# A decoder on one core: the second half's routing moved into both expert stages, and the last product rows sent directly

## The reference, cut to what matters

```python
x = _layernorm(x + _L0_attn_ref(x, ...))      # 16 heads, causal
x = _layernorm(x + _L0_xattn_ref(x, ctx_1024, ...))
x = _layernorm(x + _L0_ffn_ref(x, ...))       # experts, two of eight per token
x = _layernorm(x + _L1_attn_ref(x, ...))      # a memory matrix, updated 64 times in turn
x = _layernorm(x + _L1_xattn_ref(x, ...))     # a GELU feed-forward per sequence
x = _layernorm(x + _L1_ffn_ref(x, ...))       # experts, one of eight per token
```

```python
topk_scores, topk_idx = jax.lax.top_k(scores, k)            # first layer, k = 2
topk_probs = jax.nn.softmax(topk_scores, axis=-1)
idx = jnp.argmax(probs, axis=-1); gate = jnp.max(probs, axis=-1)   # second layer
```

## Time and profile before

| what | us |
|---|---|
| median of 3 runs (1908.21 to 1913.42) | 1910.16 |
| the profiled execution, its own time | 1911.16 |
| its span, first to last instruction | 1909.4 |

### The profile page before, as it was taken

One profiled execution on the slowest core, in us unless ns is written; L12 is line 12 of the kernel. 1 busy time (PEld: TensorE's weight loads), 2 busy tenths in 40 slices (PEclk: granted clock), 3 DMA queues, 4 the chain that ended last, 5 costly groups with the idle time before them and its releaser, 6 DMA issues. The chain is left out here.

```text
span 1909.4 us, 59731 instructions
## 1 busy us (share of the span) xinstructions
PE 1317.5 (69%) x18142; PEld 1072.6 (56%) x18196; DVE 1314.9 (69%) x4812; ACT 1104.9 (58%) x3182; POOL 1036.1 (54%) x1500
## 2 busy tenths in 40 slices
PE   6999995988878846996690999600001787849990
PEld 4677763666656636996580677400001665639990
DVE  5999995677788764542565666488886577755575
ACT  4777773677766735774472555354444565636674
POOL 2777775333326775777772344225542453867663
PEclk9999998899999978998795999855555898979995
DMA  2444442311112222333454254400000421323344
GB/s 75 106 114 106 114 115 77 107 51 50 50 42 69 79 63 73 95 91 92 126 144 146 66 111 89 82 1 1 0 1 17 149 79 51 84 70 86 89 116 118
DMA packets 201497, 152.38 MB, mean 80 GB/s; under 512 B 20482, under 2 KB 188802, under 8 KB 200962
## 3 DMA queue, kind: packets, MB, share of 16 engines
q1 hardware_dynamic: 188034, 123.13, 24.3%
q0 software_dynamic: 13312, 27.49, 4.4%
HBM read 76.54 MB, written 65.54 MB: 74 GB/s over the span
## 5 line engine op out<-in xcount | busy, mean ns | idle before, releaser
L1119 PE MATMUL ffn_run_up_ps<-ffn_run_xt,ffn_run_w_now 128*128 128x128 f32 x1792 | 248.3, 283 | 49.4 <-DVE ffn_run_h L1247 19.8
L1089 POOL DMA_INDIRECT expert_outputs<-ffn_run_y_all,ffn_run_ids x224 | 219.3, 979 | 86.8 <-issue 45.5
L1119 PEld LDWEIGHTS ffn_run_up_ps<-ffn_run_xt,ffn_run_w_now 128*128 128x128 f32 x1792 | 223.8, 196 | 61.2 <-ACT ffn_run_xt L1155 33.0
L838 POOL DMA_INDIRECT tokens_by_expert<-ffn_x_all,ffn_dest x192 | 190.7, 993 | 53.4 <-issue 49.1
L392 POOL TENSOR_TENSOR cross_k_ex<-cross_kt,k_pack 128x256 f32<-128x256 f32 x128 | 76.7, 621 | 193.0 <-ACT cross_kt L591 192.9
L1128 PE MATMUL ffn_run_y_ps<-ffn_weights,ffn_run_h 128*128 x1216 | 173.6, 277 | 0.9 <-DVE ffn_run_y_all L1264 0.5
L1599 POOL TENSOR_TENSOR recur_parts<-ffn_weights,recur_cv 128x62 f32<-128x62 f32 (+30 forms) x62 | 93.4, 1507 | 146.0 <-DVE recur_cv L1676 146.0
L1843 PE MATMUL mixer_m_ps<-mixer_mine,mem_state_coef 128*64 128x64 f32 x4 | 0.5, 334 | 246.4 <-DVE mixer_off_in L1980 246.4
L1128 PEld LDWEIGHTS ffn_run_y_ps<-ffn_weights,ffn_run_h 128*128 128x128 f32 x1216 | 154.9, 193 | 1.3 <-issue 1.3
L1156 ACT COPY ffn_run_w_now<-ffn_weights 128x512 f32 x224 | 139.4, 622 | 0.0
L1843 PEld LDWEIGHTS mixer_m_ps<-mixer_mine,mem_state_coef 128*64 128x64 f32 x4 | 0.3, 204 | 246.5 <-DVE mixer_ones L1978 246.5
(11 more groups left out here) (329 smaller groups left out, 4553.0 us busy)
## 6 DMA issues: line engine op xcount, KB each, us to landing
ffn_run_x<-tokens_by_expert SPq DMA_DIRECT2D x56, 260.0 KB, 3.0
tokens_by_expert<-fill_zeros SPq DMA_DIRECT2D x32, 292.5 KB, 2.8
ffn_run_yg<-expert_outputs SPq DMA_DIRECT2D x16, 512.0 KB, 4.6
memory_rows<-products_row SPq DMA_DIRECT2D x16, 390.0 KB, 4.5
ffn_weights<-memory_rows SPq DMA_DIRECT2D x16, 390.0 KB
tokens_by_expert<-fill_zeros SPq DMA_DIRECT2D x32, 162.5 KB, 2.6
ffn_weights<-in_pack_ffn SPq DMA_DIRECT2D x1, 4112.0 KB, 14.1
self_turned<-in_x_turned SPq DMA_DIRECT2D x64, 64.0 KB, 1.8
```

The lines of the kernel that those rows point to most:

```text
L838: pool.indirect_dma_start(xs[h], bass.IndirectOffsetOnAxis(ap=self.dest[:, r, t:t + 1], axis=0), self.x_all[:, t, :], None)\
L1089: pool.indirect_dma_start(ys, bass.IndirectOffsetOnAxis(ap=ids[:, t:t + 1], axis=0), y_all[:, t, :], None)\
L1119: mm = nc.tensor.matmul(up_ps[t.slot(2)][:, c * P:(c + 1) * P], w_now[:, t.slot(2), c * P:(c + 1) * P], xt[:, t.slot(2), :], start=True, s ...
```

## The change

The second half's routing leaves cross attention and the mixer. In `run_experts` DVE takes four of its operations per step, two ahead of the step's own first operation and two ahead of the output, from step -3 to step 15; the counts are copied and `place` begins at step 3. PE counts at the end of step 0, in an accumulator bank of its own. ACT takes the exponentials at step 3 (stage 0) or -2 (stage 1). POOL sends the outputs of tiles 0 to 7, waits for the routing (in stage 0 for the gates too), then scatters, then goes on with output 8. Three engines wait by `experts_known` for the second half's expert numbers. In stage 0 `START` goes from tile 96 to tile 108, and the roots stand nine outputs apart.

In the products the last four tiles' rows go from their buffer to `room` directly, two DMAs per tile (64 rows of 195 numbers each); the reads back come a step earlier; the wait for them moves from SP ahead of the barrier to ACT and DVE in the recurrence. ACT takes a square root at the end of the products into a column that nothing reads.

```diff
             else:
                 half_way(dve, step, 4, 4, Tile, middle, peeled=8)
                 pull(64)
-                f.route(dve, back, 1)
...
-    START = MID + (24 if top2 else 8)
+    START = MID + (36 if top2 else 8)
+    ROOTS, APART = (START + 2, 9) if top2 else (START + 5, 8)
+    EARLY = 8
...
-            for n in range(K * HALF):
-                f.scatter(pool, xs, 1, n)
             for t in range(kind.ALL):
+                if t == EARLY:
+                    pool.wait_ge(f.routed, 2)
+                    for n in range(K * HALF):
+                        f.scatter(pool, xs, 1, n)
                 pool.wait_ge(y_copied, t + 1)
...
+                if i.static and i.c == 0:
+                    f.count_tokens(pe, counts, 1)
-            skewed(pe, step, 3, 0, kind)
+            skewed(pe, step, 3, 0, kind, pause=(MID, lambda: pe.wait_ge(f.experts_known, 2)))
...
+                if i.static and i.c == (3 if top2 else -2):
+                    f.exponentials(act, 1)
...
+                if i.static and i.c == 3:
+                    pull(64, i)
+                    f.keep_counts(dve, counts, 1)
+                    routing.append(f.place(dve, 1))
+                pull(2, i)
                 t = i + 2
...
+                pull(2, i)
                 t = i
...
+                if t.exists() and t.c >= NT - 4:
+                    n, slot, uses = four(t)
+                    sp.wait_ge(row_ready, t.count())
+                    sp.wait_ge(row_copied, t.count())
+                    for b in range(2):
+                        sp.dma_start(room[2 * t.n + b:2 * t.n + b + 1, 0:S * ROW], row[b * S:(b + 1) * S, slot, t.c % 4, :]).then_inc(rows_back, 16)
...
-                t = i + -5
-                if t.exists() and t.c % 4 == 3:
+                t = i + -4
+                if t.exists() and t.c % 4 == 3 and t.c < NT - 4:
...
-            sp.wait_ge(rows_back, 16 * NT // 4)
...
+            act.activation(warm[:, :], k["half"][:, 0:1], ACT.Sqrt, scale=-1.0)
...
+            act.wait_ge(rows_back, ROWS_BACK)
             act.activation(v_len[:, :], flat[:, VV + 1:VV + 1 + (S - 1) * (ROW + 1) + 1:ROW + 1], ACT.Sqrt).then_inc(squares, 1)
...
+            dve.wait_ge(rows_back, ROWS_BACK)
```

More of the change, by code:

```diff
@@ L554, in _ @@
                 pe.wait_ge(summed, NT)
-                f.count_tokens(pe, back, 1)
         @block.scalar
@@ L626, in _ @@
                 half_way(act, step, 4, 6, Tile, middle, peeled=8)
-                f.exponentials(act, 1)
         @block.vector
@@ L893, in keep_counts @@
         cp.then_inc(self.counts_read, 1)
-    def route(self, dve, counts, h):
-        for _ in self.select(dve, h):
-            pass
-        self.keep_counts(dve, counts, h)
-        for _ in self.place(dve, h):
-            pass
     def place(self, dve, h):
@@ L943, in place @@
         yield from link(ts(self.expert_f[:, 1, :], self.expert_f[:, 0, :], float(E_N - 1), None, ALU.min))
-        yield from link(dve.tensor_copy(self.expert_of[:, h * (T // 2):(h + 1) * (T // 2)], self.expert_f[:, 1, :]))
+        dve.tensor_copy(self.expert_of[:, h * (T // 2):(h + 1) * (T // 2)], self.expert_f[:, 1, :]).then_inc(self.experts_known, 1)
+        yield
         if self.top2:
@@ L1003, in run_experts @@
         xt_ps, up_ps, y_ps = ([ps(f"{n}{i}", [P, 512]) for i in range(2)] for n in ("xt", "up", "y"))
+        counts = ps("counts", [P, 512])
         loaded = [sem(f"x_loaded{i}") for i in range(2)]
@@ L1090, in _ @@
                     .then_inc(stored[t // MID], 16)
-                u, part = (t - START) // 8, (t - START) % 8
-                if t >= START and part == 5 and u < 4:
+                u, part = (t - ROOTS) // APART, (t - ROOTS) % APART
+                if t >= ROOTS and part == 0 and u < 4:
                     root(2 * u)
@@ L1172, in step @@
                         norm(2 * u + (part - 4) // 2, (0, 1) if part % 2 == 0 else (2, 3))
-            half_way(act, step, 3, 0, kind, MID)
+            half_way(act, step, 3, 0, kind, MID - 8, lambda: act.wait_ge(f.experts_known, 2))
             for u in range(4):
@@ L1227, in shifts, with pull @@
                     .then_inc(shift_ready, 1)
+            routing = [f.select(dve, 1)]
+            def pull(n, i):
+                for _ in range(n if i.static and i.c < 16 else 0):
+                    next(routing[-1], None)
             def step(i):
                 e_now, e_ahead = (None, None) if top2 else look(i)
+                if i.static and i.c == 3:
[3 more added lines that the diff above has]
+                pull(2, i)
                 t = i + 2
@@ L1280, in _ @@
             dve.wait_ge(numbered, 2)
-            half_way(dve, step, 3, 0, kind, MID)
+            half_way(dve, step, 3, 0, kind, MID - 8, lambda: dve.wait_ge(f.experts_known, 2), peeled=16)
             if START + 32 + 3 >= kind.ALL:
@@ L1300, with memory_products @@
 N_MEM = float(F * D)
-def memory_products(nc, stage, k, x_in, w_all, w_norm, eta, rows_out, room, k_all, v_all, qt_all, eta_col):
+def memory_products(nc, stage, k, x_in, w_all, w_norm, eta, rows_out, rows_back, room, k_all, v_all, qt_all, eta_col):
     with ExitStack() as ctx:
@@ L1316, in memory_products @@
         eta_neg = sb("eta_neg", [P, 1])
+        warm = sb("warm", [P, 1])
         x = sb("x", [P, 2, 4, D])
@@ L1354, in step @@
                 t = i + -1
-                if t.exists() and t.c % 4 == 3:
+                if t.exists() and t.c >= NT - 4:
[4 more added lines that the diff above has]
+                        sp.dma_start(room[2 * t.n + b:2 * t.n + b + 1, 0:S * ROW], row[b * S:(b + 1) * S, slot, t.c % 4, :]).then_inc(rows_back, 16)
+                elif t.exists() and t.c % 4 == 3:
                     n, slot, uses = four(t)
@@ L1370, in step @@
                     sp.dma_start(x[:, slot, :, :], x_v[n]).then_inc(loaded[slot], 16)
-            for c in range(-11, NT + 5):
+            for c in range(-11, NT + 1):
                 step(kind(0, c))
-            for s in stored:
-                sp.wait_ge(s, 16 * NT // 8)
-            sp.wait_ge(rows_back, 16 * NT // 4)
+            for n, s in enumerate(stored):
+                sp.wait_ge(s, 16 * (NT // 8 - n))
         @block.gpsimd
@@ L1562, in _, with memory_recurrence @@
             skewed(dve, step, 4, 1, kind)
-def memory_recurrence(nc, stage, k, room, coef, offset):
+ROWS_BACK = 16 * (NT // 4 - 1 + 8)
+def memory_recurrence(nc, stage, k, room, rows_back, coef, offset):
     with ExitStack() as ctx:
@@ L1916, in _ @@
             half_way(pe, step, 6, 3, Eights, middle)
-            f.count_tokens(pe, counts, 1)
         @block.scalar
@@ L2055, in _ @@
             pull(64)
-            f.route(dve, counts, 1)
 def build(nc, a, out):
@@ L2087, in build @@
             run_experts(nc, f, k, xs[0], ys[0], x1)
+        rows_back = ctx.enter_context(nc.semaphore("rows_back"))
         rows = nc.dram_tensor("memory_rows", (B * S, ROW), F32, kind="Internal").ap()
@@ L2094, in build @@
                 k_all, v_all, qt_all = mm.sb("k_all", [P, NT, F]), mm.sb("v_all", [P, NT, D]), mm.sb("qt_all", [P, NT, P])
-                memory_products(nc, "products", k, x1, part["w_all"], part["w_norm"], part["eta"], rows, f.weights, k_all, v_all, qt_all, eta[:, :])
-                memory_recurrence(nc, "recur", k, f.weights, coef, offset[:, :])
+                memory_products(nc, "products", k, x1, part["w_all"], part["w_norm"], part["eta"], rows, rows_back, f.weights, k_all, v_all, qt_all, eta[:, :])
+                memory_recurrence(nc, "recur", k, f.weights, rows_back, coef, offset[:, :])
                 memory_and_mixer(nc, "mixer", k, x1, flat(a["ctx_1024"]), k_all, v_all, qt_all, eta[:, :], part["w_out_t"], coef, offset[:, :], f, xs[1])
```

3 lines of the change are left out of this document (1 added, 2 removed).

## The result

The changed kernel takes 1932.56 us (median of 4 runs, 1932.48 to 1935.52) against 1911.79 for the kernel before, a ratio of 1.012 with a 95% interval of 1.010 to 1.014. It is 21 us slower; 17 were forecast (1927, range 1906 to 1937). The profiled execution took 1932.48 us, its span 1930.7.

The account below looks back on a forecast made before the run. POOL's list was taken to bound expert stage 0, PE the second half of stage 1. Terms 16 - 10 + 11 = +17 on the profiled 1911.16 gave 1928, less 1.0 for the median: 1927 us, range 1906 to 1937.

Parts of the forecast that it names:

- The bound of stage 0: Expert stage 0 goes by POOL's list; its first scatter goes out 26.4 us later, its last output 16 us later.
- the eight early outputs: Stage 0, POOL: eight outputs sent ahead of the first scatter needn't be sent later, 8 x 1.28 = 10.2 us.
- The products' term: Products to recurrence: with one read back left, the first root comes 10 us earlier (ends 12 and 5).
- should land by then: End of products: tile 63's direct rows, issued at 1223.7, land by the time the read back does, 1232.8.
- The sentence beside it: Products: descriptors go in ring order, so direct rows would wait for the read back; gain nearer 5 to 8 than 10.
- Stage 1: Expert stage 1, bounded by PE in its second half: 11 us later (4 to 15), with 0.8 gained at its start.
- the ramp: Stage 1, first steps: DVE waits for the exponentials behind a table load, put at 2.3 us.
- the first sums: Stage 1: their fetch must wait for POOL's outputs and lands about 1819, DVE arriving at 1812: some 6 us more.
- Rival 2: Barriers at 723 and 1697: POOL's drain is long only because DVE routes beside it; 1905 us, chance 0.12.
- Rival 1: Both expert stages: the routing fits DVE's idle time, gates about 24 us behind stage 0's start; 1915 us, chance 0.20.
- Rival 3: Stage 0: second half's rows come too late for tile 72; 10 us and more, 1938 to 1945, chance 0.08.
- Rival 4: Barriers: the drain grows to fill the removed routing, 5 us less gained; 1932, sharing the forecast's 0.60.

Follow-up runs that it names:

- prod_split: Kernel before with only the products' part, stores ahead of neighbouring reads back, and the last read back issued two steps earlier; ratio 0.9978 to the kernel before.

## Why the prediction was right, and which terms were off

- **The bound of stage 0** and its sum were right: 16 us later at POOL's last output, measured 15.7. Start 721.5 (721.5), gates 32.3 behind it (31.0), first scatter 754.7 (753.57), last output near 1020 (1018.7). The two runs with other orders on POOL confirm it from both sides: DVE's work unchanged, the stage moves with POOL's head start alone. DVE's loss in the steps came partly from elsewhere than the prediction said: ACT's two table loads around the exponentials made DVE wait 1.80 us at step 3 (the row of 740.16 above), which I had not priced for stage 0. That wait lies ahead of the gates, so it is not hidden; but from the output of tile 2 to the gates DVE took 15.9 us with it, where 17.2 had been put without it.
- **What the prediction did not see** is that the new order has a price of its own. It put the eight early outputs down as 10.2 us that needn't be sent later. Beside late gates that was right (9.1 measured). But with the gates there, POOL loses 13.5 us by waiting for the same outputs.
- **The products' term was mis-sized**: 10 forecast, 5.7 measured here, 4.8 in the mean of the four profiles that have it. Two steps failed. The read back, put down as issued "about 1222.4", 1.2 us ahead of the last product row, came 3.1 us behind it, because SP was held by a store that took 11.0 us. And the direct rows, which "should land by then", don't, even with the read back on time: in prod_split it went out 3.3 us ahead of the last product row, yet half of the last two tiles' rows began only at 9.1 and the first root stood 16.6 behind. The sentence beside it, from the Trainium skill, page "DMA: Bandwidth & Descriptors", section "Queues, rings and completion order", gave 5 to 8 by ring order, and the time came out at the low end of that or just under it; the stores (10.2 us behind a read back, 5.1 ahead of it) agree with it. But the direct rows waited on ACT's queue too, which ring order on SP's doesn't explain.
- **Stage 1** was forecast at 11, of which 0.8 were to be gained at its start: 11.8 from the start on. From there POOL's last output came 12.9 later (13.3 in the mean of three profiles) and the end 13.7: the ramp was 3.2 us where I put 2.3, the first sums waited 6.4 where I put 6, and the tail took 0.8 more. The 0.8 at the start were not there: the stage begins 5.3 us behind the mixer's last scatter before and after.
- **Rival 2** (the drain shrinks without the routing beside it) is out: the drain of cross attention ends at 717.7, and at 717.8 with stage 0 alone changed, 5.3 us behind the last scatter as before. The mixer's drain still ends 2.7 us behind its last scatter. Something of it is in the trace all the same: the last six scatters of cross attention stand 1.39 us apart beside the routing and 1.26 without it, which makes 0.6 us. **Rival 1** (routing hidden) is out: the gates came at 31, not 24. **Rival 3** is out: the second half's rows were sent by 837, and around tile 72 PE waited no longer than before. Rival 4 doesn't arise: the 5.4 us were gained.
- The sum was 17, the profiles gave 21.3: 4.3 of the difference from the products. The rest nearly cancels, and that is luck: stage 1 took 1.9 more than forecast from its start on, while it began 1.6 earlier against the first root than forecast, by spread.
- Slips in the working move nothing: the drain's far bound is 10.4 (723.0 - 712.6), not 10.3; direct rows landing at 1237, with the 2 us of preparation behind them, would give 6, not 5; and the 5 for stage 0 in the sum of the low ends isn't worked out.

## What to carry to other kernels

When one engine's list bounds a stage, ask of an edit only where that list gets idle time: here a list that hardly waited was made to wait at its head, and no hiding elsewhere paid for it. Putting work that must still be produced ahead of work that is ready costs that engine the wait; putting it into a wait that is there anyway is a gain. And a transfer issued a step earlier may push back the one behind it that someone waits for.

## What the runs showed of the hardware that I had not expected

A store of 390 KB took 10.2 us where a read back stood ahead of it, 5.1 where it stood behind. Packets of 780 B took 38 to 40 ns in the median into DRAM. Into one partition those issued by ACT took 48 to 50 for the half that ran at once and 115 to 143 for the half that ran behind the read back, and 281 where all tiles went that way. Half the packets of such a DMA ran within 2.5 us and half waited some 9 us for the read back, from SP's queue and from ACT's alike. A drain on POOL ended 5.3 us behind the last indirect DMA of cross attention and 2.7 behind the mixer's, with DVE busy beside it or not.
